# A two-layer conditional adapter kernel: tile 1's A bank from rounded parts, and the start-up order of five engines around it

## The reference

```python
x = x + einsum('bct,bcd->bdt', x, w0[conditions])          # layer 0: a 64 x 64 matrix picked per sample
H = einsum('btd,od->bto', x, W)                             # layer 1: one 512 x 512 matrix for all
xa = einsum('btd,brd->btr', x, A[adapter_idx])              # rank 16, 8 adapters
delta = einsum('btr,bor->bto', xa, Bm[adapter_idx]) * s[adapter_idx]
x = x + H + delta
```

## Time and profile before

| | us |
|---|---|
| median of 3 runs | 77.06 (77.06, 77.06, 78.25) |
| the profiled execution, its own time | 76.92 |
| its span | 75.2 |
| PE busy | 71.0 (94% of the span) |
| DVE busy | 55.6 (74%) |
| ACT busy | 51.5 (68%) |
| POOL busy | 33.2 (44%) |

### The profile page before, as it was taken

The page is one execution under the profiler, slowest core; times in us unless marked ns, Lnnn a source line. Parts: engine busy times, 40 slices in busy tenths (PEclk is TensorE's granted clock), DMA queues, the critical chain, the costliest instruction groups (busy, mean ns, idle before and its releaser), DMA issues.

```text
span 75.2 us, 1943 instructions
## 1 busy us (share of the span) xinstructions
PE 71.0 (94%) x468; PEld 65.7 (87%) x468; DVE 55.6 (74%) x143; ACT 51.5 (68%) x126; POOL 33.2 (44%) x76
## 2 busy tenths in 40 slices
PE   5999997999999999999999999999999999999940
PEld 5988986786999999999999999999999999999930
DVE  3019896896989777979797959887797949765920
ACT  0737884985979686886668666867697867566440
POOL 5700799697954283456245720690258320000000
PEclk9999999999999999999999999999999999999999
DMA  0999388794669756887957897578416440303025
GB/s 0 268 417 384 92 239 246 168 280 164 210 221 277 256 157 221 243 269 243 293 191 223 244 310 196 153 200 277 158 40 242 137 146 0 139 13 139 0 99 180
DMA packets 9677, 14.55 MB, mean 193 GB/s; under 512 B 3650, under 2 KB 4418, under 8 KB 9666
## 3 DMA queue, kind: packets, MB, share of 16 engines
q1 hardware_dynamic: 7554, 9.16, 37.3%
q0 software_dynamic: 1536, 4.20, 18.6%
q10 hardware_dynamic: 576, 1.07, 4.2%
HBM read 10.23 MB, written 4.19 MB: 192 GB/s over the span
## 4 chain that ended last, share of the span: by engine, by line
PE 90%; DVE 4%; ACT 1%; issue 1%
PE z_ps L654 54%; PE z_ps L642 8%; PE v_ps L723 5%; PE out_ps L696 5%; PE out_ps L709 4%; PE out_ps L710 4%; PE out_ps L714 4%; PE v_ps L688 2%; PE out_ps L702 2%; DVE moving L495 2%; PE v_ps L685 1%; ACT moving L343 1%; DVE out_sb L629 1%; ACT z_plain L373 1%; DVE low_rank L537 0%
## 5 line engine op out<-in xcount | busy, mean ns | idle before, releaser
L654 PE MATMUL z_ps<-moving,x_high 128*128 128x272 f32 x224 | 33.5, 289 | 0.0
L654 PEld LDWEIGHTS z_ps<-moving,x_high 128*128 128x128 f32 x224 | 29.9, 188 | 0.7
L290 POOL DMA_DIRECT2D b_raw<-b_t x32 | 16.2, 507 | 13.6 <-DMA a_scales<-a_t 4.6
L654 PE MATMUL z_ps<-moving,x_low 128*128 128x272 f32 x112 | 18.6, 287 | 0.0
L654 PEld LDWEIGHTS z_ps<-moving,x_low 128*128 128x128 f32 x112 | 15.8, 188 | 0.0
L511 DVE TENSOR_TENSOR z_low<-z_ps,z_high 128x272 fp32r<-128x272 f32 (+1 forms) x28 | 11.8, 423 | 1.9 <-ACT z_high L364 1.0
L283 POOL CAST moving<-a_table 128x128 fp32r x28 | 8.4, 330 | 10.8 <-PE z_ps L654 10.6
L380 ACT ACTIVATE b_high<-b_raw,group_sb 128x512 fp32r<-128x512 f32 x16 | 11.4, 715 | 0.0
L394 ACT ACTIVATE v_high<-v_ps,group_sb 128x128 fp32r<-128x128 f32 x16 | 5.9, 368 | 8.0 <-PE v_ps L688 7.9
L520 DVE TENSOR_TENSOR b_stack<-b_raw,b_high 128x512 fp32r<-128x512 f32 x16 | 11.0, 690 | 0.4 <-ACT b_high L380 0.4
L364 ACT ACTIVATE z_high<-z_ps 128x272 fp32r<-128x272 f32 (+1 forms) x28 | 10.5, 376 | 0.2
(11 more groups left out here) (58 smaller groups left out, 77.8 us busy)
## 6 DMA issues: line engine op xcount, KB each, us to landing
b_raw<-b_t POOLq DMA_DIRECT2D x32, 128.0 KB, 3.2
out<-out_sb SPq DMA_DIRECT2D x15, 256.0 KB, 3.3
x_raw<-xt SPq DMA_DIRECT2D x13, 256.0 KB, 3.8
w_sb<-w SPq DMA_DIRECT2D x32, 16.0 KB, 3.3
w_late<-w_late_t SPq DMA_DIRECT2D x1, 480.0 KB, 6.3
head<-head_c ACTq DMA_DIRECT2D x1, 400.0 KB, 4.2
head<-head_d SPq DMA_DIRECT2D x1, 384.0 KB, 5.2
head<-head_a ACTq DMA_DIRECT2D x1, 264.0 KB, 2.9
```

The costliest lines, as they stand in the source:

```text
L290: pool.dma_start(b_raw[s * C:(s + 1) * C, t % BBUFS, :], b_t[ds(which[s], 1), :, :].rearrange("a r (g n) -> (a r) g n", g=1) .to_broadcast ...
L654: last = nc.tensor.matmul(z_bank(t, part), x[:, t % XBUFS, k * P:(k + 1) * P], moving[:, int(n == HL), k, at:at + HALF], start=((n, k) == ...
```

## The change

Tile 1's A bank is no longer plain: it is made of the 12 products of rounded parts, in the order HH, HL, LH, with x of tile 1 rounded by ACT (`high_of_x(1)`) and its rest taken by DVE (`low_of_x(1)`), and with tile 1's A columns cast by POOL (`take_a(1)`) into the last 32 columns of `moving`, which tile 2 uses too. So `take_a(2)` now waits until tile 1's A bank is done (`plain_bank_done[1]`), and `take_raw_a(1)` on ACT is gone. `take_a(1)` stands on POOL ahead of `add_identity(1)` and `load_b(2)`, and `add_identity` of batch 2 now stands ahead of `load_b(3)`, behind `take_a(2)`. DVE's list becomes: low part of `a_table`, `low_of_w(2)`, `take_low_rank(0)`, `low_of_w(3)`, `low_of_x(1)`, `low_of_v(0)`, `low_of_z(2, W)`, `low_of_b(0)`, and on as before. On ACT the high part of `a_table` moves ahead of the last two pieces of W. On PE only HH of tile 2's W bank stands ahead of tile 0's A bank; LH and HL stand behind it. `x_low` and `x_high` for tile 1 are strided views, since tile 1's x lies in two pieces of `head`; `x_count(t)` is the place of tile t in the order in which x is rounded (2, 1, 3, 4, ...).

```diff
 POOL
-                at = 0 if t % 2 else AC + OUT
+                at = 0 if t % 2 and t > 1 else AC + OUT
+                if t == 2:
+                    pool.wait_ge(plain_bank_done[1], 1)
...
             add_identity(0)
+            pool.wait_ge(a_ready, 1)
+            take_a(which[1], 1)
             add_identity(1)
             load_b(which[2], 2)
-            pool.wait_ge(a_ready, 1)
             take_a(which[2], 2)
+            add_identity(BATCH_OF[3])
             load_b(which[3], 3)
-            add_identity(BATCH_OF[3])
             take_a(which[3], 3)
 ACT
             take_z(1, W_PART)
+            act.wait_ge(a_scaled_ready, 1)
+            nc.scalar.activation(a_table[:, :, 0, :], a_scaled[:], ACT.Copy).then_inc(a_high_ready, 1)
             high_of_w(2)
             high_of_w(3)
-            take_raw_a(1)
-            act.wait_ge(a_scaled_ready, 1)
-            nc.scalar.activation(a_table[:, :, 0, :], a_scaled[:], ACT.Copy).then_inc(a_high_ready, 1)
+            high_of_x(1)
             take_z(0, A_PART)
 DVE
-            low_of_w(2)
-            low_of_w(3)
             dve.wait_ge(a_high_ready, 1)
             nc.vector.tensor_tensor(out=a_table[:, :, 1, :], ..., op=ALU.subtract).then_inc(a_ready, 1)
+            low_of_w(2)
             dve.wait_ge(own_rank_ready, 2 + PER)
             take_low_rank(0)
+            low_of_w(3)
+            low_of_x(1)
+            low_of_v(0)
             low_of_z(2, W_PART)
-            low_of_v(0)
             low_of_b(0)
 PE, in products
+                    if t < PLAIN and (n, k) == (HL, 0):
+                        pe.wait_ge(w_low_ready, len(PIECES))
 PE, the list
-            w_bank(2, 0, 2 * K)
+            w_bank(2, 0, K)
...
             plain_products(0, A_PART, without_diagonal_first[3:]).then_inc(plain_bank_done[0], 1)
+            w_bank(2, K, 2 * K)
             pe.wait_ge(w_low_ready, 2)
             w_bank(2, 2 * K, 3 * K)
             weigh_low_rank(0)
-            pe.wait_ge(raw_cols_ready, 2 * PER)
-            plain_products(1, A_PART, without_diagonal_first).then_inc(plain_bank_done[1], 1)
+            pe.wait_ge(w_high_ready, len(PIECES))
+            pe.wait_ge(a_cols_ready, PER)
+            products(1, A_PART, LOW_X_LAST).then_inc(plain_bank_done[1], 1)
             plain_layer0(0)
             weigh_low_rank(1)
-            pe.wait_ge(w_low_ready, len(PIECES))
             a_bank(2)
```

More of the change, by code:

```diff
@@ L48, in adapted_residual_kernel @@
     BANK_AT = (BANK - HALF, 0)
-    RAW_A = (AC + LATE, 0)
     HH, HL, LH = 0, 1, 2
     PRODUCTS = [(n, k) for n in (HH, LH, HL) for k in range(K)]
+    LOW_X_LAST = [(n, k) for n in (HH, HL, LH) for k in range(K)]
     ROWS = (K - 1, *range(K // 2, K - 1), *range(0, K // 2))
@@ L97, in adapted_residual_kernel @@
         warmed = sb("warmed", [1, 1], fp32)
-        head = sb("head", [P, HEAD_AT[-1]], fp32)
-        w_late = sb("w_late", [P, K, AC + LATE + AC], fp32)
+        head = sb("head", [P, X_AT[1][0] + 2 * X1_STEP], fp32)
+        w_late = sb("w_late", [P, K, LATE + AC], fp32)
         moving = sb("moving", [P, 2, K, ROW], fp32r)
@@ L185, in x_of, with x_part @@
         def x_of(t):
+            if t == 1:
+                both = head[:, X_AT[1][0]:X_AT[1][0] + 2 * X1_STEP].rearrange("p (h n) -> p h n", h=2)
+                return both[:, :, 0:X_HALF]
             return head[:, X_AT[t][0]:X_AT[t][0] + WIDTH] if t < EARLY else x_raw[:, t - EARLY, :]
+        def x_part(parts, t):
+            to = parts[:, t % XBUFS, :]
+            return to.rearrange("p (h n) -> p h n", h=2) if t == 1 else to
         def w_rows(p):
@@ L192, in w_rows @@
             if c0:
-                return w_late[:, k0:k1, AC:AC + LATE]
+                return w_late[:, k0:k1, 0:LATE]
             return head[:, W_AT[p]:W_AT[p] + 2 * HALF].rearrange("p (k n) -> p k n", k=K // 2)
@@ L198, in w_block @@
             if c0 >= HALF:
-                return w_late[:, k, AC + c0 - HALF:AC + c1 - HALF]
+                return w_late[:, k, c0 - HALF:c1 - HALF]
             at = W_AT[k // (K // 2)] + k % (K // 2) * HALF
@@ L243, in _ @@
             sync.dma_start(head[:, HEAD_AT[3]:HEAD_AT[4]], head_d).then_inc(head_loaded[3], 16)
-            sync.dma_start(w_late[:, :, AC:AC + LATE], w_late_t).then_inc(w_late_loaded, 16)
+            sync.dma_start(w_late[:, :, 0:LATE], w_late_t).then_inc(w_late_loaded, 16)
             sync.wait_ge(index_loaded, 16)
@@ L331, in _ @@
             act.wait_ge(index_loaded, 16)
-            first = read_indices(act, 1, 0, ADAPTERS, PLAIN)
+            first = read_indices(act, 1, 0, ADAPTERS, 1)
             def high_of_w(p):
@@ L346, in take_raw_a @@
             def take_raw_a(t):
-                at = RAW_A[t]
+                at = LATE
                 for s in range(PER):
@@ L383, in high_of_x @@
             def high_of_x(t):
-                act.wait_ge(x_loaded[t - 2], 16)
+                if t == 1:
+                    act.wait_ge(head_loaded[1], 16)
+                    act.wait_ge(head_loaded[3], 16)
+                else:
+                    act.wait_ge(x_loaded[t - 2], 16)
                 if t >= PLAIN + XBUFS:
                     act.wait_ge(w_bank_done, t - XBUFS + 1)
-                nc.scalar.activation(x_high[:, t % XBUFS, :], x_of(t), ACT.Copy).then_inc(x_high_ready, 1)
+                nc.scalar.activation(x_part(x_high, t), x_of(t), ACT.Copy).then_inc(x_high_ready, 1)
             def high_of_v(t):
@@ L486, in low_of_x @@
             def low_of_x(t):
-                dve.wait_ge(x_high_ready, t - PLAIN + 1)
-                nc.vector.tensor_tensor(out=x_low[:, t % XBUFS, :], in0=x_of(t),
-                                        in1=x_high[:, t % XBUFS, :].bitcast(fp32),
+                dve.wait_ge(x_high_ready, x_count(t))
+                nc.vector.tensor_tensor(out=x_part(x_low, t), in0=x_of(t),
+                                        in1=x_part(x_high, t).bitcast(fp32),
                                         op=ALU.subtract).then_inc(x_low_ready, 1)
@@ L531, in take_low_rank @@
                     dve.wait_ge(rank_parts_ready, t - PLAIN)
-                at = 0 if t < PLAIN and RAW_A[t] == 0 else A_AT
-                u = z_ps[t % 2][:, A_BANK[side(t)], at:at + AC]
+                u = z_ps[t % 2][:, A_BANK[side(t)], A_AT:A_AT + AC]
                 if t < PLAIN:
@@ L639, in plain_products @@
                 for n, k in ks:
-                    at = min(RAW_A[t], AC)
-                    w = w_late[:, k, at:at + LATE + AC] if part == A_PART else w_block(k, 0, HALF)
+                    w = w_late[:, k, :] if part == A_PART else w_block(k, 0, HALF)
                     last = nc.tensor.matmul(z_bank(t, part), x_block(t, k), w, start=(n == 0), stop=(n == K - 1))
```

14 lines of the change are left out of this document (8 added, 6 removed).

## The result

The change makes the kernel slower, by 1.5% in one set of executions and 0.8% in another. Four executions of the changed kernel gave 78.0 us as their median (77.7 to 78.85), beside 77.17 for the kernel before (77.06 to 78.25); the ratio is 1.0153 with a 95% interval from 1.0105 to 1.020. A second set of ten executions gave 77.66 beside 77.27, ratio 1.0083 (1.0036 to 1.0129). Ratios here compare the undisturbed executions of both kernels on one chip, so they need not be the quotient of the medians. Forecast were 76.6 us and a range of 75.9 to 77.4: the sign is wrong and the time lies outside.

A forecast was written before the change was run, and what follows sets the result against it. PE was taken to bound the kernel, its list freeing 0.68 + 0.35 = 1.03 us, of which POOL's moved wait left 0.48. 76.92 - 0.48 = 76.44, plus 0.14 for the median: 76.6 us, range 75.9 to 77.4.

The forecast's parts named there:

- What bounds the kernel: From 18.77 us on PE's own work makes the end, as long as POOL, ACT and DVE keep up.
- S: Start of `weigh_low_rank(2)` on PE, forecast at 17.90 in place of 18.38.
- The wait ahead of `weigh_low_rank(0)`: PE's start-up: idle 0.42 us and the latency of an unpipelined start go, 0.68 us gained.
- Tile 1's A bank: PE: 12 products of rounded parts take 1.49 us where 8 plain instructions take 1.84, 0.35 us less.
- signs of being wrong: Include the addition ending beyond 16.2 or at 15.5, PE waiting for `moving`, or a loop stall behind 19 us.
- This is the term that decides: POOL's `take_a(2)`, held for tile 1's A bank, delays batch 2's addition; 0.48 us gained of 1.03 freed.
- E: End of POOL's `add_identity` of batch 2 (tiles 2 and 3), forecast at 15.75, bounds 15.48 and 16.4.
- E + 2.15: PE's start of `weigh_low_rank(2)`: 2.15 us behind that addition's end, through ACT and DVE, so 17.90.
- Rival (c): Slower at POOL's `take_a(2)`: casts and addition fall into DVE differences, addition ends 16.9, time 77.7; chance 0.12.
- Each instruction waits for the other engine's to end: DVE and POOL at SBUF take turns, then work their own 0.55 us (DVE) or 0.15 (cast).

The follow-up runs named there:

- the repeat: The changed kernel run once more, unchanged: 77.66 us, its profiled execution 78.41 us.
- the rounded parts alone: The changed kernel with DVE, ACT and PE back in the old order around tile 0's masking: 78.81 us, ratio 1.0203.
- its loop apart: The changed kernel with only later additions (tiles 4 and 5 on) placed between the two halves of a load_b: 77.71 us, ratio 1.0032.

## Why the prediction was wrong

**What bounds the kernel: right.** From S on PE alone makes the end. That the other engines keep up behind it stood in the prediction as a condition, with a price of nothing. In four traces it did not hold: 57.7 us follow S in the repeat, with all casts on ACT, with tile 1's casts held, and with the rounded parts alone (77.7 - 20.03 in the last two). In the other traces it is 56.8 to 57.2.

**The wait ahead of `weigh_low_rank(0)`, 0.68 us: 0.09 came.** It ended at 12.73 in place of 12.82. The step that failed here is the time of `low_of_w(2)` ahead of the masking: I took 1.1 us from 10.1, it was 1.48 from 10.54. The start is 0.4 later as the head's transfer landed 0.37 later, which a profile of one execution doesn't bound. The length is the turns: I had counted one of POOL's instructions against it, and the change itself puts casts behind the addition, so that two or more fell in. In the repeat it took 0.90 and the masking ended at 11.92, ahead of its need at 12.49, as PE was later there; the first pair of `weigh_low_rank` still ended only at 12.70.

**Tile 1's A bank, 1.84 to 1.49 us: 1.81.** The 12 products need no more than 1.49 of PE, but HL waited for W's last low part (13.10 in place of 12.3) and LH for the low part of x (13.70 in place of 13.05). With all casts on ACT it ran from 12.49, the end of the product ahead of it, to 14.01: 1.52 us, the count. Its end came at 14.53 in place of 13.75. In the repeat the wait was another, for tile 1's casts on POOL: I had them done by 12.2 at the latest and they ended at 12.64. That is one of the signs of being wrong that the prediction names, a wait of PE for `moving` ahead of tile 1's bank.

**"This is the term that decides": right, and mis-sized.** This is the step that made the forecast wrong. The form E + 2.15 holds: the changed kernel's first trace has 2.08, and five others in which PE idles ahead of S have 2.24 or 2.25. The price of E was wrong. I had 15.75; it was 16.92: 0.78 from the bank's late end, 0.12 from the start of the casts behind it (14.70 - 14.53 against 13.80 - 13.75), 0.27 from the casts (1.07 against 0.8). With S = 19.00 in place of 17.90, a gain of 0.48 us became a loss of 0.62. From the last cast to E it took 1.15 us as I had it, but as one addition that lost its turn, not as a wait for the transfer and a turn. The bank's end and E are tied: 2.39 us apart in the first trace and 2.30 or 2.31 in the four others that keep wait and casts on POOL with the addition behind them. I had them 2.00 apart. My forecast thus hung on three favourable readings in a row (the masking at 11.4, the bank at 13.75, the casts beside an instruction that reads PSUM), each near its good end. Rival (c), E = 16.9 and 77.7 us, named place, price and the DVE instructions that the casts and the addition fall into; the profiled execution took 77.7, the median was 78.0. Its condition, `load_b(2)` through only at 13.9 as tile 1's casts lost both turns, did not hold in the first trace (13.53, and POOL idled 1.17 for PE), so that its number fits there is in part luck; it held in the repeat (14.45). It had 0.12 and deserved more, since the earlier trace rows already held casts of 1.45 and an addition of 1.22.

**"Each instruction waits for the other engine's to end": wrong as turns.** The rows I played out happened to alternate. Where POOL has several reads queued, DVE can stand through all of them: 1.85 us against 1.22 of POOL's work in three traces, 1.94 against four instructions in one. The Trainium skill, page "SBUF — State Buffer", section "Who interferes with whom", says that the later of the two is blocked until the first is done; the traces agree on the blocking, and show that the wait isn't limited to one instruction of the other engine. On the order they do not agree as far as the starts in the rows tell: the difference of 1.85 us started at 19.52, POOL's first cast at 19.59, and it was the difference that stood.

**What stays open.** The kernel before idles 0.42 and 0.34 us ahead of `weigh_low_rank(0)` in its two traces, where its first banks ended at 8.6. In eight of the other fourteen they ended at 9.1 to 9.5, and in none of those eight was the idle time there over 0.15 us. Whether the 0.42 stands in the kernel before when its transfers are late was not seen: both of its traces are of executions (76.92 and 76.85 us) below the medians of its larger sets, 77.03 to 77.47, and what the longer ones lose no trace shows. That the changed kernel with its loop apart has S 0.80 us later than the earlier trace rows and a median only 0.24 above fits with such a loss in the kernel before. How much of the loss is the wait on POOL and how much the casts' own time is open too, as the first trace has 1.17 us of wait and the repeat 0.20 at nearly the same E. And who wins the first turn (0.47 or 0.90 us for the same addition) changed from one execution to the next for no reason that the traces show. Separate columns for tile 1, which would let POOL cast without any wait and with the right result, were not tried.

## What to carry to other kernels

When a transform moves to a shared buffer, price the whole queue that it enters, the wait and the work: here 0.35 us off PE's list put two casts of 1.0 us and a wait of 0.20 to 1.17 us ahead of an addition on which ACT, DVE and PE depend in turn. Put a wait on an in-order engine where what stands behind it has cover of its own, or on another engine, as ACT's two casts did (ratio 0.9921 with all work done). And before cutting a stall of 0.4 us at the start of a kernel, take more than one trace: the head's transfers moved the first banks by up to 1.2 us.

## What the hardware showed that I had not expected

- GpSimd instructions that read SBUF, queued back to back, can hold a VectorE difference of two SBUF inputs through all of them: 1.85 us in place of 0.69 (two casts, one addition), 1.94 in place of 0.65 (two additions, two casts). A difference that had started 0.27 us ahead of a single addition was held too and took 1.58 us; two traces have this seven times, at 1.57 or 1.58. In all these cases the difference ended 0.53 to 0.56 us after GpSimd's last read.
- The first addition on POOL took 0.47 us in six traces and 0.87 to 0.90 in six others: whoever gets the first turn differs from run to run.
- ScalarE made the same pair of casts in 0.50 to 0.51 us at every place, beside DVE or not; GpSimd took 0.53 to 1.53.
